# Turning the attention heads by DMA instead of by TensorE in a gated cross-attention kernel, with new instruction orders

## What is computed

```python
xn = layernorm(ctx, ln1_w, ln1_b);  ln = layernorm(layernorm0(x), ln2_w, ln2_b)
q = (ln @ Wq) * (1 + side) + side;  k, v = split(xn @ Wkv)          # 16 heads x 64
attn = softmax(q @ k.T / 8);        o = attn @ v                     # o: 112 x 1024
x = x + tanh(g_x) * (o @ Wout)
x = x + tanh(g_f) * ffn(layernorm0(x))   # 256 -> 1024 -> 256; activations rounded to 8 bits, weights to -1, 0, 1
```

## Time and profile before

| | |
|---|---|
| median of 3 runs | 1130.98 us (1130.7 to 1131.45) |
| profiled execution | 1132.53 us, its span 1130.7 us |
| busy, share of the span | PE 94%, ACT 86%, DVE 84%, POOL 69% |
| share of the 16 DMA engines | q1: 64.2% |
| mean granted TensorE clock | 0.981 of full speed |

### The profile page before, as it was taken

One profiled execution on the slowest core, in us unless ns is written; L12 is line 12 of the kernel. 1 busy time (PEld: TensorE's weight loads), 2 busy tenths in 40 slices (PEclk: granted clock), 3 DMA queues, 4 the chain that ended last, 5 costly groups with the idle time before them and its releaser, 6 DMA issues.

```text
span 1130.7 us, 32113 instructions
## 1 busy us (share of the span) xinstructions
PE 1067.6 (94%) x11900; PEld 733.8 (65%) x11900; DVE 945.4 (84%) x2108; ACT 970.6 (86%) x1864; POOL 776.6 (69%) x839
## 2 busy tenths in 40 slices
PE   2789999999999999999999999999999999999983
PEld 1456666676676676767667666766776676667662
DVE  2688789888889888888988878898888888888984
ACT  4588789999999979999999979999999978999862
POOL 4376667766777777676787766678767767877732
PEclk9799999999999999999999999999999999999986
DMA  8246665676776666679666676756666775765741
GB/s 274 52 95 109 105 103 100 121 117 118 114 138 103 107 117 113 120 110 139 113 101 127 118 116 100 133 112 100 128 109 119 118 136 99 102 127 101 120 107 38
DMA packets 409498, 129.42 MB, mean 114 GB/s; under 512 B 391136, under 2 KB 404192, under 8 KB 409344
## 3 DMA queue, kind: packets, MB, share of 16 engines
q1 hardware_dynamic: 409344, 127.36, 64.2%
HBM read 26.71 MB, written 3.67 MB: 27 GB/s over the span
## 4 chain that ended last, share of the span: by engine, by line
PE 73%; ACT 8%; issue 5%; DMA 4%; DVE 4%; POOL 3%; POOLq 1%; DVEq 1%; SPq 0%; ACTq 0%
PE work L833 15%; PE work L834 15%; PE work L835 15%; PE ps_s L852 10%; DMA pt<-pn 4%; PE ps_o L833 3%; PE ps_o L835 3%; PE ps_o L834 3%; ACT prob L606 2%; PE work L916 2%; PE work L945 2%; ACT q_f L572 2%; PE work L907 2%; PE work L954 2%; ACT L606 2%
## 5 line engine op out<-in xcount | busy, mean ns | idle before, releaser
L447 POOL TENSOR_TENSOR pn<-prob,pn 112x750 f16<-112x750 f32 x256 | 399.3, 1565 | 115.7 <-ACT pn L616 104.6
L606 ACT ACTIVATE prob<-ps_s,neg_max 112x375 f32<-112x375 f32 x512 | 265.2, 573 | 9.0 <-DVE neg_max L748 7.1
L748 DVE TENSOR_REDUCE neg_max<-ps_s 112x2 f32<-112x750 f32 x256 | 237.2, 928 | 24.0 <-PE ps_s L852 24.0
L833 PE MATMUL work<-z,wkv_h 128*128 128x375 f16 x512 | 168.2, 328 | 15.1 <-DVE k_l L673 8.7
L833 PE MATMUL ps_o<-v_h,pt 128*128 128x65 f16 (+1 forms) x1536 | 168.3, 195 | 8.8 <-DMA pt<-pn 5.6
L834 PE MATMUL ps_o<-v_l,pt 128*128 128x65 f16 (+1 forms) x1536 | 168.1, 193 | 0.0
L835 PE MATMUL ps_o<-v_h,pt 128*128 128x65 f16 (+1 forms) x1536 | 168.0, 194 | 0.0
L835 PE MATMUL work<-z,wkv_l 128*128 128x375 f16 x512 | 167.0, 326 | 0.0
L834 PE MATMUL work<-z,wkv_h 128*128 128x375 f16 x512 | 166.9, 326 | 0.0
L529 ACT ACTIVATE k_h<-work 128x375 f16<-128x375 f32 x256 | 121.4, 487 | 50.8 <-PE work L835 45.7
L673 DVE SCALAR_TENSOR_TENSOR k_l<-work,k_h 128x375 f16<-128x375 f32 x256 | 136.0, 540 | 33.6 <-ACT k_h L529 33.5
(11 more groups left out here) (133 smaller groups left out, 2725.1 us busy)
## 6 DMA issues: line engine op xcount, KB each, us to landing
ctx_in<-in_ctx SPq DMA_DIRECT2D x32, 375.0 KB
pt<-pn SPq DMA_TRANSPOSE x256, 3.4
x_in<-in_x SPq DMA_DIRECT2D x32, 112.0 KB, 3.8
x_res<-in_x SPq DMA_DIRECT2D x28, 128.0 KB, 5.2
out<-y SPq DMA_DIRECT2D x28, 128.0 KB, 2.0
stage<-in_wkv SPq DMA_DIRECT2D x2, 1024.0 KB, 9.3
stage<-in_w SPq DMA_DIRECT2D x2, 1024.0 KB, 10.5
stage<-in_wq SPq DMA_DIRECT2D x1, 1024.0 KB, 8.5
```

The lines of the kernel that those rows point to most:

```text
L447: g.tensor_tensor(buf[:, 1, :, 0:SK], prob[:, p % 2], buf[:, 0, :, 0:SK], ALU.subtract).then_inc(p_lo, 1)
L606: i = a.activation(prob[:, p % 2, h, :], ps_s[0:SQ, 2 * (p % 2) + h, 0:SK], ACT.Exp, bias=neg_max[:, 2 * (p % 2) + h:2 * (p % 2) + h + 1])
L748: v.tensor_reduce(neg_max[:, 2 * (p % 2):2 * (p % 2) + 2], ps_s[0:SQ, 2 * (p % 2):2 * (p % 2) + 2, 0:SK], X, ALU.max, negate=True).then_in ...
L833: t_.matmul(dst, sh, mh, start=(n == 0), stop=False)
```

## The change

- The heads are no longer turned on TensorE. OH (ACT) copies half of `attn` (112 x 512, float32, in SBUF) to a float16 high part in a new tile `an`; a new step OL (POOL) subtracts to the low part; OT is now a DMA transpose of that half of `an`, both parts, into `ot`, issued by SP. WO waits for the DMA. OO0, OO1 and the DVE step OT are gone, with their two jobs a batch in the `work` banks. N waits, from batch 1 on, for OL of the batch before, since `attn` has one buffer.
- ACT casts pairs 0 and 4 only; DVE casts the other six.
- The last two tiles, not only the last, are turned on TensorE in the feed-forward part (`TAIL = 2`).
- In the beginning the late weights are loaded by a step LW of their own, behind LD of batch 1; the split of the K weights is halved (WKH1, WKH0, WKL1, WKL0) and the first ZS1 runs on DVE.
- FIRST, ORDER and LAST of all five engines are new.

```diff
-CAST_ACT = (0, 2, 4, 6)
+TAIL = 2
+CAST_ACT = (0, 4)
...
 ORDER["PE"] = [
...
+    ("A5", -1), ("S2", 0), ("S3", 0), ("K0", 1), ("K1", 1), ("A6", -1), ("F0", -2), ("A7", -1),
+    ("K2", 1), ("F1", -2), ("V11", 0), ("V10", 0), ("V12", 0), ("K3", 1), ("S4", 0), ("S5", 0),
+    ("K4", 1), ("A0", 0), ("WO", -1), ("A1", 0), ("Z1", 2), ("F2", -3), ("Q0", 1), ("S6", 0),
+    ("S7", 0), ("K7", 1), ("A2", 0), ("K5", 1), ("A3", 0), ("Z0", 2), ("K6", 1), ("S0", 1),
+    ("S1", 1), ("V02", 1), ("V01", 1), ("A4", 0), ("V00", 1), ("Q1", 1), ("ZX", 2),
 ]
...
 ORDER["POOL"] = [
...
+    ("PL6", -1), ("HQ", -3), ("PL7", -1), ("ZS0", 1), ("PL0", 0), ("LNA", 2), ("QS1", 0), ("OL0", -1),
+    ("PL1", 0), ("OL1", -1), ("PL2", 0), ("PL3", 0), ("ZXS", 1), ("XB", -2), ("PL4", 0), ("RM1", -1),
+    ("PL5", 0), ("QS0", 1), ("RM2", -2), ("ZS1", 2), ("XQ", -1),
 ]
 ORDER["SP"] = [
...
+    ("LD", 3), ("OT0", -1), ("OT1", -1), ("T1", 0), ("LX", 3), ("ST", -4), ("T2", 0), ("T3", 0),
+    ("T4", 0), ("T5", 0), ("XD", -1), ("T6", 0), ("T7", 0), ("RS", 0), ("T0", 1), ("HD", -2),
 ]
 FIRST["SP"] = [
-    ("LX", 1), ("LD", 1), ("LD", 2), ("LX", 2), ("T0", 0), ("T1", 0), ("T2", 0), ("LX", 3),
...
+    ("LX", 1), ("LD", 1), ("LW", 0), ("LD", 2), ("LX", 2), ("T0", 0), ("LX", 3), ("LD", 3),
...
 FIRST["DVE"] = [
-    ("BA", 0), ("BB", 0), ("BS", 0), ("WKL", 0), ("WQL", 0), ("BA", 1), ("KL1", 0), ("BB", 1),
...
+    ("BA", 0), ("BB", 0), ("BS", 0), ("WKL1", 0), ("WKL0", 0), ("ZS1", 0), ("WQL", 0), ("KL0", 0),
+    ("BA", 1), ("KL1", 0), ("BB", 1), ("BS", 1), ("WVL", 0), ("KL3", 0), ("KL4", 0), ("KL2", 0),
...
+            def turn_heads(b, half):
+                sp.wait_ge(o_lo, 2 * b + half + 1)
+                if b == 0:
+                    sp.wait_ge(lo_split[3], 1)
+                for t in last_user(b):
+                    sp.wait_ge(full[BANK["WO", t]], USE["WO", t])
+                sp.dma_start_transpose(ot[:, half].rearrange("p a c q -> p (a c) q")[:, :, columns(b)],
+                                       an[half][:].rearrange("p a n -> p (a n)")).then_inc(o_turned[half], 16)
...
+            def split_heads(b, half):
+                pool.wait_ge(o_hi, 2 * b + half + 1)
+                g.tensor_tensor(an[half][:, 1], attn[:, half * HALF:(half + 1) * HALF], an[half][:, 0], ALU.subtract).then_inc(o_lo, 1)
...
                 if name[0:2] == "OH":
...
-                    a.activation(ot[:, half, 0, :, columns(b)],
-                                 work[:, BANK[job], 0:4 * SQ].rearrange("p (c q) -> p c q", c=4), ACT.Identity).then_inc(o_hi, 1)
+                    half = int(name[2])
+                    act.wait_ge(o_normed, 4 * b + 2 + 2 * half)
+                    if b > 0:
+                        act.wait_ge(o_turned[half], 16 * b)
+                    a.activation(an[half][:, 0], attn[:, half * HALF:(half + 1) * HALF], ACT.Identity).then_inc(o_hi, 1)
...
+                if b > 0:
+                    dve.wait_ge(o_lo, 2 * b + quarter // 2 - 1)
                 v.tensor_tensor(attn[:, quarter * D:(quarter + 1) * D].rearrange("p (h d) -> p h d", d=DH),
...
-                if name in ("OO0", "OO1"):
-                    pe.wait_ge(o_normed, 4 * b + 2 + 2 * int(name[2]))
-                    for m in range(4):
-                        c = 4 * int(name[2]) + m
-                        i = t_.transpose(w[:, m * SQ:(m + 1) * SQ], attn[:, c * P:(c + 1) * P], ident[0:SQ, 0:SQ])
...
-                    for half in ("OO0", "OO1"):
-                        results(last_batch(b), [half])
+                    for half in range(2):
+                        pe.wait_ge(o_turned[half], 16 * (last_batch(b) + 1))
```

More of the change, by code:

```diff
@@ L32 @@
 RING = 7 * P
-CAST_ACT = (0, 2, 4, 6)
+TAIL = 2
+CAST_ACT = (0, 4)
 ORDER, FIRST, LAST = {}, {}, {}
 ORDER["PE"] = [
[6 rows of a table removed]
[5 rows of a table added]
 ]
 FIRST["PE"] = [
[11 rows of a table removed]
[12 rows of a table added]
 ]
 LAST["PE"] = [
[12 rows of a table removed]
[12 rows of a table added]
 ]
 ORDER["ACT"] = [
[5 rows of a table removed]
[5 rows of a table added]
 ]
 FIRST["ACT"] = [
-    ("LNW", 0), ("WKH", 0), ("ZF1", 0), ("ZF0", 0), ("ZXF", 0), ("WQH", 0), ("KH1", 0), ("WVH", 0),
[11 rows of a table removed]
[11 rows of a table added]
 ]
 LAST["ACT"] = [
[11 rows of a table removed]
[11 rows of a table added]
 ]
 ORDER["DVE"] = [
[6 rows of a table removed]
[6 rows of a table added]
 ]
 FIRST["DVE"] = [
[9 rows of a table removed]
[11 rows of a table added]
 ]
 LAST["DVE"] = [
[14 rows of a table removed]
[15 rows of a table added]
 ]
 ORDER["POOL"] = [
-    ("XB", -2), ("HQ", -3), ("XQ", -2), ("PL1", 0), ("QS1", 0), ("LNA", 2), ("PL2", 0), ("PL3", 0),
-    ("ZXS", 1), ("PL4", 0), ("RM2", -2), ("PL5", 0), ("RM1", -1), ("QS0", 1), ("ZS0", 2), ("PL6", 0),
-    ("ZS1", 2), ("PL7", 0), ("PL0", 1),
[3 rows of a table added]
 ]
 FIRST["POOL"] = [
[5 rows of a table removed]
[5 rows of a table added]
 ]
 LAST["POOL"] = [
[6 rows of a table removed]
[7 rows of a table added]
 ]
 ORDER["SP"] = [
-    ("LX", 4), ("T4", 1), ("T5", 1), ("T6", 1), ("ST", -2), ("T7", 1), ("T0", 2), ("XD", 0),
-    ("HD", -1), ("T1", 2), ("LD", 5), ("T2", 2), ("RS", 1), ("T3", 2),
+    ("LD", 3), ("OT0", -1), ("OT1", -1), ("T1", 0), ("LX", 3), ("ST", -4), ("T2", 0), ("T3", 0),
+    ("T4", 0), ("T5", 0), ("XD", -1), ("T6", 0), ("T7", 0), ("RS", 0), ("T0", 1), ("HD", -2),
 ]
 FIRST["SP"] = [
[6 rows of a table removed]
[4 rows of a table added]
 ]
 LAST["SP"] = [
[5 rows of a table removed]
[6 rows of a table added]
 ]
-START, END = -5, B + 4
+START, END = -3, B + 4
 TOKEN_STEPS = ("WO", "XT", "HT", "F0", "F1", "F2", "XR", "GE", "SQ", "HR", "X1", "XST", "SC1", "XTE", "HE0", "HE1", "HMX", "SC2",
@@ L284, in build @@
         attn = sb("attn", [SQ, INNER])
+        an = [sb(f"an{i}", [SQ, 2, HALF], F16) for i in range(2)]
         x_res, x1 = sb("x_res", [P, D]), sb("x1", [P, D])
@@ L324, in build @@
         o_normed, o_hi, q_ready = sem("o_normed"), sem("o_hi"), sem("q_ready")
+        o_lo = sem("o_lo")
+        o_turned = [sem(f"o_turned{i}") for i in range(2)]
         block = st.enter_context(nc.Block())
@@ L350, in load_queries @@
                     sp.dma_start(x_in[:], x[b]).then_inc(x_loaded, 16)
-                if b == 1:
-                    load_late_weights()
             def load_late_weights():
@@ L394, in _ @@
                     turn(b, int(name[1]))
-                if name == "XD" and b < NT - 1:
+                if name[0:2] == "OT":
+                    turn_heads(b, int(name[2]))
+                if name == "XD" and b < NT - TAIL:
                     turn_quantised(b)
-                if name == "HD" and b < NT - 1:
+                if name == "HD" and b < NT - TAIL:
                     turn_hidden(b)
@@ L402, in _ @@
                     load_queries(b)
+                if name == "LW":
+                    load_late_weights()
                 if name == "RS":
@@ L482, in step @@
                     split_p(b, int(name[2]))
+                if name[0:2] == "OL":
+                    split_heads(b, int(name[2]))
                 if name[0:2] == "QS":
@@ L486, in step @@
                     split_zx(b)
-                if name in ("ZS0", "ZS1"):
+                if name == "ZS0" or name == "ZS1" and b > 0:
                     split_z(b, int(name[2]))
@@ L532, in step @@
                 job = (name[0] + name[2:], b)
-                if name == "WKH":
-                    split_hi(0, wk_in, wkv_f[:, :, 0:INNER], wkv_h[:, :, 0:INNER])
+                if name in ("WKH0", "WKH1"):
+                    c = slice(int(name[3]) * HALF, (int(name[3]) + 1) * HALF)
+                    split_hi(0, wk_in, wkv_f[:, :, c], wkv_h[:, :, c])
                 if name == "WQH":
@@ L555, in step @@
                 if name[0:2] == "OH":
-                    job, half = ("OO" + name[2], b), int(name[2])
-                    act.wait_ge(full[BANK[job]], USE[job])
-                    if b == 0:
-                        act.wait_ge(lo_split[3], 1)
-                    for t in last_user(b):
-                        act.wait_ge(full[BANK["WO", t]], USE["WO", t])
-                    a.activation(ot[:, half, 0, :, columns(b)],
-                                 work[:, BANK[job], 0:4 * SQ].rearrange("p (c q) -> p c q", c=4), ACT.Identity).then_inc(o_hi, 1)
+                    half = int(name[2])
[3 more added lines that the diff above has]
+                    a.activation(an[half][:, 0], attn[:, half * HALF:(half + 1) * HALF], ACT.Identity).then_inc(o_hi, 1)
                 if name[0:2] == "QF":
@@ L643, in _, with split_lo @@
             v = nc.vector
-            def split_lo(n, w, hi_part, lo_part):
-                dve.wait_ge(hi_split[n], 1)
+            def split_lo(n, w, hi_part, lo_part, count=1):
+                dve.wait_ge(hi_split[n], count)
                 for k in range(w.shape[1]):
@@ L650, in split_lo, with split_z_first @@
                 i.then_inc(lo_split[n], 1)
+            def split_z_first():
```

(28 more changed lines are left out.)

## The result

| | before | after |
|---|---|---|
| median | 1130.84 us (1130.37 to 1132.17) | 1139.85 us (1136.45 to 1142.32, 6 runs) |
| ratio to before | 1 | 1.0079, 95% interval 1.0061 to 1.0096 |
| profiled execution, span | 1132.53, 1130.7 us | 1142.32, 1140.5 us |
| mean granted TensorE clock | 0.981 | 0.977 |

The change makes the kernel 0.8% slower. The forecast was 1096 us, 3% faster. The profiled execution of the kernel after is the slowest of its six, 2.5 us above their median; that of the kernel before is 1.5 us above its own.

The account below looks back on a forecast made before the run. TensorE was taken to bind for about 1000 us, the other engines following. Span 1130.7 - 28 (loop) - 9 (beginning) - 0 (end) + 2 (casts) = 1095.7, so 1096 us; forecast 1084 to 1106 (0.62), 8 in 10 range 1080 to 1118.

Parts of the forecast that it names:

- Beginning, -9: Start of the kernel: earlier context load, less low clock and an earlier first K gain 9 us, between 3 and 12.
- TensorE loses OO, 28 us of the loop: Loop: 64 OO jobs of 0.44 us leave TensorE, so 28 us leave the span, upper bound 37.
- the 32.5 that I forecast: Loop: a turn (one batch) should fall from 33.4 to 32.5 us.
- Hidden with 2 to 3 us to spare: Loop: the heads' way from N3 to WO, about 6.5 us, hides behind some 9 us of TensorE work.
- My bound of 8.6 for the landing: Loop, heads' DMA transpose: landing taken as 3.3 us, 3.1 to 8.6 in `pn`'s rows; at 8.6 it would show.
- The casts, 2 us: Loop: six DVE casts meeting POOL's instructions cost 2 us of stalls in all, from 0 to 20.
- rival 2: Loop: DVE's casts meet POOL each time, turn near 34.3 us, 1150 us in all; chance 0.08.
- rival 2's threshold of 0.75 a cast: Loop: rival 2 decides from 0.75 us a cast, DVE's slack (33.4 - 28.9) divided by six casts.
- The end, 0: End: WO 3.1 us later, covered by 2.9 us of HMX slack and 1 us at YE; net 0, -1 to +5.
- the condition that I had named: End: if WO starts after an idle TensorE at the lower clock level, 24 matmuls of 0.11 us double.
- rival 3: Loop: T1 to T7 and WO wait for DMA landings, the 28 us come back, 1124 us or no change; chance 0.07.

Follow-up runs that it names:

- x7: Kernel before with only the load of the second context moved ahead of the late weights in the beginning: 1118.68 us, ratio 0.9903 to before.
- x14: x11 with one VectorE step, HMX (row maximum of the hidden layer), moved behind KL3 and KL4: 1109.63 us, ratio 0.9816 to before.
- x16: x14 plus new end orders: WO(31) right behind A7(31) on TensorE, X1(31) and XST(31) ahead of HE1(30) on DVE: 1112.64 us, ratio 0.9845.
- x11: Kernel after with the edits of x12 and x3 together: 1116.18 us, ratio 0.9874 to before.
- x1: Kernel after with casts 2 and 6 back on ACT, so four casts there: 1141.52 us, ratio 1.0098 to before.
- x13: x11 with four casts of a batch on ACT instead of two: 1125.86 us, ratio 0.9962 to before.
- x12: Kernel after with two context tiles normalised in place, the context load issued behind T5 of the turn before: 1136.95 us, ratio 1.0064 to before.
- x3: Kernel after with the six DVE casts written as a maximum over an axis of length 1: 1127.63 us, ratio 0.9969 to before.
- x2: Kernel after with the context load issued behind OT0, OT1 and T1 instead of ahead of them: 1244.48 us, ratio 1.1016 to before.

## Why the prediction was wrong

**Beginning, -9: right.** -8.2 in the kernel after; x7 shows that the load's place gives 10.0 of it, so to that point the rest of the new beginning (the split of Z on two engines, the halved K weights), for which I counted 2 us, gave back nearly 2; at batch 8 the kernel after is 1.4 us ahead of x7 (299.8 against 301.2), which is less than x14 and x16 differ there.

**TensorE loses OO, 28 us of the loop: the step that failed.** The jobs are gone, and where few waits are left (x11, x14) PE is busy 5.4 to 5.9 us less in eight turns, against 7.0 by 0.44 a job. What failed is the inference from it: "what leaves its stream there leaves the span, if the other engines can follow", which I tested by the engines' sums, all at 0.82 to 0.89. x1 and x13 take 30 and 41 us of 800 from DVE and gain nothing or lose; x12 takes WO's wait from TensorE and the turn with a token tile stays. What decides is the length of each closed round of hand-overs that returns one turn later. Two were at 33.5 (x3's chain, over the heads' DMA) and 33.9 (x12's, over DVE and POOL), above the 32.5 that I forecast. I never summed a round from WO to WO. With both shortened (x11) the mean of eight turns is 32.7 us, and in x14 32.6, of which TensorE is busy 32.1 in both; the forecast's 0.9 off the mean of 33.1 is 32.2. My 33.4 was a turn with a token tile, not the mean, so my 23.95 turns in 800 us should have been 24.2; nothing hangs on that.

**"Hidden with 2 to 3 us to spare": mis-sized.** The way from N3 to WO was put at 6.5 us with a landing of 3.3, taken from the earlier trace rows; without N3's own 0.9 that is 5.6, and it was 8.8, with 5.7 for the landing and 1.0 from N3 to OH on ACT where I had some 0.5 for all hand-overs. OL 1.16 and OH 0.64 were right. My bound of 8.6 for the landing was in the text, with "would show", and it should have been priced at the place: SP's new list has a load of 375 KB right ahead of OT0. x2 and x12 show 2.7 us without it.

**The casts, 2 us: mis-sized.** I set the stalls at 2, from 0 to 20; taking the lock away gives 12 us (x3), with the heads' round still in the way. The means were 925 ns a cast, so 0.38 over 0.54, below rival 2's threshold of 0.75 a cast, and yet the turn went over. The threshold was a sum over DVE, while the cast sits in a round with POOL: DVE's cast waits for POOL, and POOL's next instruction waits for that cast. My sum also put the two new casts at the median of 542 ns, where the mean of the kernel before was 627.

**The end, 0: the way right, its cover wrong.** I had 5.5 us from N3 to WO. In x16, where WO stands first, it is 5.3 (attn ends 1067.5, WO starts 1072.7), against 2.4 in the earlier trace rows. In the kernel after it is 8.1, from N3's end at 1104.03, for ahead of WO on TensorE stand F2(28), whose hidden tile (24) still goes by DMA, and F1(30), and both waited:

```profile
1106.65 1.87 PE L976 MATMUL work<-w_t,stage 128*128 128x256 f16 x8 [3.57 <-DVE stage L830]
...
1110.50 1.86 PE L967 MATMUL work<-w_t,xqt 128*128 128x512 f16 x4 [1.77 <-DVE xqt L817]
1112.16 0.42 PE L860 MATMUL work<-wout_h,stage 128*128 128x256 f16 x1
```

Then the condition that I had named came true: after these waits the granted clock is 0.50 from 1112.2 to 1115.1, the lower of its two levels, and 14 of WO's 24 matmuls start 0.21 us apart instead of 0.11. From N3's end to WO's end are 12.4 us, 5.2 before. Against these 7.2 stand 2.0 us less from the batch's first maximum to N3, and only 1.4 less behind WO, where I had 2.9 of slack and 1 more. The end's +3.8 is within the -1 to +5 given.

**The rivals.** What happened is rival 2's mechanism and, for the heads' transposes, rival 3's, at once: taking them away gives 12 and 3 us alone and 24 together. I had given them 0.08 and 0.07 as if one excluded the other, and each its own time (1150, 1124). Both signs of rival 2 came, the casts' mean over 0.9 us and POOL's idle time before L464. Rival 3's sign was the landing's median over 5 us, which came for `an`, but `pt`'s stayed at 3.4. The Trainium skill's preference for TensorE over a DMA transpose (VectorE: DVE Perf Modes; "Rules for kernel authors"), which I set aside, came true for the change as made. x11 and x14 say that it need not: with the heads on DMA as well, batch 8 to 31 take 737.5 and 733.2 us against 746.2 before. What their other casts and second context tile would give with the heads on TensorE was not tried.
